# Attention of a two-layer kernel: head pairs, two-part fp32r operands and output groups of 256 queries

## What is computed

```python
qs = (x @ wq_sem).reshape(b, sl, H, DS)          # H = 16 heads, DS = DG = 64, DV = 128
ksem = (x @ wk_sem).reshape(b, sl, H, DS)
qg = _rope((x @ wq_geo).reshape(b, sl, H, DG))
kg = _rope((x @ wk_geo).reshape(b, sl, H, DG))
v = (x @ wv).reshape(b, sl, H, DV)
```

## Time and profile before

| | |
|---|---|
| median of 3 runs | 1966.86 us |
| the profiled execution | 1968.04 us, span 1966.4 us |
| PE busy / PE weight loads | 1781.5 us (91%) / 1315.6 us (67%) |
| DVE / ACT / POOL busy | 1106.4 us (56%) / 972.0 us (49%) / 802.1 us (41%) |
| mean granted clock of TensorE | 0.956 of full speed |

### The profile page before, as it was taken

The page is one execution under the profiler, slowest core; times in us unless marked ns, Lnnn a source line. Parts: engine busy times, 40 slices in busy tenths (PEclk is TensorE's granted clock), DMA queues, the critical chain, the costliest instruction groups (busy, mean ns, idle before and its releaser), DMA issues. The chain is left out here.

```text
span 1966.4 us, 33208 instructions
## 1 busy us (share of the span) xinstructions
PE 1781.5 (91%) x9018; PEld 1315.6 (67%) x9018; DVE 1106.4 (56%) x2157; ACT 972.0 (49%) x2052; POOL 802.1 (41%) x788
## 2 busy tenths in 40 slices
PE   6399988439999999999999999999999999999998
PEld 2256656427777777777777777777776677677777
DVE  4799953695546455554645454555544333334467
ACT  4599923015555555555555455555554344444322
POOL 1489931333433444343434434443432233222354
PEclk9599999559999999999999999999999999999999
DMA  4753258200000000000000000000101999999623
GB/s 138 287 183 105 98 154 261 84 3 20 9 20 16 21 8 19 16 20 7 16 21 8 19 16 21 8 19 16 39 9 31 286 313 314 308 315 321 192 87 97
DMA packets 99216, 192.94 MB, mean 98 GB/s; under 512 B 15332, under 2 KB 59620, under 8 KB 96596
## 3 DMA queue, kind: packets, MB, share of 16 engines
q1 hardware_dynamic: 57684, 108.76, 18.0%
q0 software_dynamic: 17152, 47.67, 7.5%
q10 hardware_dynamic: 24336, 35.98, 5.5%
HBM read 140.84 MB, written 51.51 MB: 98 GB/s over the span
## 5 line engine op out<-in xcount | busy, mean ns | idle before, releaser
L1175 POOL TENSOR_TENSOR sw<-sw,rope_t 64x512 f32<-64x512 f32 x128 | 164.3, 1283 | 611.9 <-ACT sw L995 611.9
L1078 DVE TENSOR_TENSOR t<-ps,rope_t 128x512 f32<-128x512 f32 x128 | 88.5, 692 | 363.5 <-ACT sw L995 363.4
L890 PE MATMUL ps<-pt,v 128*128 128x512 f32 (+3 forms) x768 | 270.1, 495 | 19.8 <-DVE xr L1095 17.8
L987 ACT ACTIVATE pb<-ps,negmax 128x128 f32<-128x128 f32 (+7 forms) x256 | 191.1, 747 | 177.1 <-DVE negmax L1063 177.0
L1063 DVE TENSOR_REDUCE negmax<-ps 128x1 f32<-128x128 f32 (+7 forms) x256 | 191.9, 750 | 78.1 <-PE ps L849 76.1
L890 PEld LDWEIGHTS ps<-pt,v 128*128 128x128 f32 x768 | 139.1, 191 | 121.4 <-issue 79.5
L541 POOL DMA_DIRECT2D w2r<-in_w x148 | 77.5, 523 | 326.1 <-PE ps L590 306.3
L1178 POOL TENSOR_TENSOR t<-t,sw 64x512 f32<-64x512 f32 x128 | 179.1, 1399 | 33.6 <-POOL sw L1175 17.9
L883 PE MATMUL ps<-ident,pb 128*128 128x128 f32 x1152 | 171.3, 276 | 23.6 <-ACT pb L987 23.4
L974 ACT COPY pt<-ps 128x512 f32<-128x512 f32 (+3 forms) x256 | 130.1, 508 | 102.0 <-PE ps L883 94.5
L883 PEld LDWEIGHTS ps<-ident,pb 128*128 128x128 f32 x1152 | 133.8, 141 | 68.1 <-ACT pb L987 45.1
(11 more groups left out here) (198 smaller groups left out, 3677.2 us busy)
## 6 DMA issues: line engine op xcount, KB each, us to landing
w13r<-in_w SPq DMA_DIRECT2D x124, 352.0 KB, 6.0
w2r<-in_w POOLq DMA_DIRECT2D x148, 176.0 KB, 6.0
result<-yy ACTq DMA_DIRECT2D x148, 128.0 KB, 5.1
crow<-c_rows SPq DMA_DIRECT2D x32, 512.0 KB, 3.6
t<-sorted SPq DMA_DIRECT2D x124, 128.0 KB, 5.5
sorted<-zeros ACTq DMA_DIRECT2D x15, 1024.0 KB, 16.9
hc<-in_w SPq DMA_DIRECT2D x24, 352.0 KB, 5.3
wraw<-in_wqkv SPq DMA_DIRECT2D x16, 384.0 KB, 3.3
```

The source lines that it names most:

```text
L890: last = pe.matmul(ps[:, 6, c0:512], v[:, buf, j], pt[g][:, j, c0:512], start=j == 0, stop=j == 4 * g + 3)
L987: act.activation(pb[:, qt % 2, 0:cols], ps[:, bank:bank + 2, :].rearrange("p a n -> p (a n)")[:, 0:cols], ACT.Exp, bias=negmax[:, par, qn: ...
L1175: g.tensor_tensor(sw[64:128, p % 2, :], sw[64:128, p % 2, :], rope_t[64:128, 1, (p // 2) * 512:(p // 2 + 1) * 512], ALU.mult).then_inc(s_t ...
```

## The change

The loop goes over pairs of heads, and inside a pair over four iterations c: sequence 0 with both heads, then sequence 1 with both heads (`hh` = c % 2 is the head within the pair, 1 the second one). There are still 32 iterations of eight steps, and maxima, exps, scores, transposes and pieces are as many and as large as before.

- Values are projected for both heads of a pair and 256 tokens at a time, in the iterations with hh = 0, steps 0, 1, 4 and 7, by `three` on the split x and split weights (12 matmuls of 256 columns each time).
- Probabilities are rounded to fp32r by ScalarE (all chunks, `ptr`), and VectorE subtracts to get the second part (`ptl`). A transpose chunk may overwrite its bank once that subtraction is done (`s_pl`). ScalarE does exp of tile qt + 1 before the copies of tile qt.
- Outputs are made in four groups of 256 queries per iteration, by `three`; each is rounded on ScalarE, split on VectorE, projected by `three` with a split wo, and added. All of it goes through bank 6, at fixed steps.
- The subtraction `rest` moves from VectorE to GpSimd, where it comes after the rotation of the following piece.
- Weights of the second head of a pair have their own slot; values and wo are split too. The loads are reordered accordingly.
- The ring buffer `w2r1` of the experts no longer has room of its own beside the attention's buffers; GpSimd waits for the end of attention before it loads it.

The core of the diff (lines removed from the printed functions are left out; "..." marks cuts):

```diff
+        early = {"w13r1": sbk("w13r1", [P, RING, DC, 2 * INNER]), "xs1": t1[:].rearrange("p a (b d) -> p (a b) d", d=D)}
...
+        vr = sbo("vr", [P, 8, 2 * P], F32R)
+        vl = sbo("vl", [P, 8, 2 * P], F32R)
+        ptr = [sbo("ptr0", [P, 6, 2 * P], F32R), sbo("ptr1", [P, 8, 2 * P], F32R)]
+        ptl = [sbo("ptl0", [P, 6, 2 * P], F32R), sbo("ptl1", [P, 8, 2 * P], F32R)]
...
+            def values(m, b, fill):
+                pe.wait_ge(s_e7, fill - 1)
+                for a in range(2):
+                    t0 = b * SEQ + (2 * m + a) * P
+                    o = ps[:, 7, a * 2 * P:(a + 1) * 2 * P]
                     for c in range(DC):
...
+                        last = three(pe, o, xnr[:, c, t0:t0 + P], xnl[:, c, t0:t0 + P], wvr[:, c], wvl[:, c], c == 0, c == DC - 1)
+                last.then_inc(s_b7, 1)
...
             def transposes(it, qt):
                 w(pe, s_exp, 8 * it + qt + 1)
                 for ci, j0, j1 in chunks(qt):
...
+                    w(pe, s_pl, CHUNKS * it + ci - 1)
                     for j in range(j0, j1):
                         last = pe.transpose(ps[:, 4 + ci % 2, (j - j0) * P:(j - j0 + 1) * P], pb[:, qt % 2, j * P:(j + 1) * P], ident[:])
                     last.then_inc(s_T, 1)
...
+            def output(it, g, hh):
+                w(pe, s_e6, output_fill(it, g) - 1)
+                pe.wait_ge(s_pl, CHUNKS * it + (2, 4, 8, 12)[g])
+                hd = slice(hh * P, (hh + 1) * P)
+                for j in range(2 * g + 2):
+                    c0 = P if j == 2 * g + 1 else 0
+                    last = three(pe, ps[:, 6, c0:2 * P], vr[:, j, hd], vl[:, j, hd], ptr[g % 2][:, j, c0:2 * P], ptl[g % 2][:, j, c0:2 * P],
+                                 j == 0, j == 2 * g + 1)
+                last.then_inc(s_b6, 1)
+            def project_out(it, g, slot):
+                pe.wait_ge(s_e6, project_fill(it, g) - 1)
                 for a in range(2):
...
+                    sl = slice(a * P, (a + 1) * P)
+                    last = three(pe, ps[:, 6, a * D:(a + 1) * D], otr[:, sl], otl[:, sl], wor[:, slot], wol[:, slot], True, True)
                 last.then_inc(s_b6, 1)
...
+            def body(hp, c, last):
+                it, pair = 4 * hp + c, 2 * hp + c // 2
+                b, hh = c // 2, c % 2
+                next_b = ((c + 1) % 4) // 2
                 for qt in range(8):
                     transposes(it, qt)
                     if qt < 6:
...
+                        scores(it, qt + 2, hh)
                     elif not last:
...
+                        scores(it, qt + 2, 1 - hh)
+                    if qt == 0 and not first(it):
+                        if hh == 1:
+                            pe.wait_ge(s_e7, value_fill(pair, 3))
+                        output(it - 1, 3, 1 - hh)
+                    if qt == 1 and not first(it):
+                        project_out(it - 1, 3, 1 - hh)
+                    if qt in (2, 4, 6):
+                        output(it, qt // 2 - 1, hh)
+                    if qt in (3, 5, 7):
+                        if qt == 3 and b == 0:
+                            pe.wait_ge(s_wos, 2 * hp + hh + 1)
+                        project_out(it, qt // 2 - 1, hh)
+                    if qt in VALUE and hh == 0:
+                        if qt == 0 and b == 0:
+                            pe.wait_ge(s_wvs, hp + 1)
+                        values(VALUE[qt], b, value_fill(pair, VALUE[qt]))
+                    if qt in PIECE and not last:
+                        p = PIECE[qt]
+                        if qt == 2 and next_b == 0:
+                            pe.wait_ge(s_ws, 2 * hp + c // 3 * 2 + (1 - hh) + 1)
+                        piece(p, next_b, 1 - hh, piece_fill(pair, hh, p))
             heads_loop(pe, body)
...
             def probs(it, qt):
...
+                for ci, j0, j1 in chunks(qt):
+                    act.wait_ge(s_T, CHUNKS * it + ci + 1)
+                    g = qt // 2
+                    if qt % 2 == 0 and j0 == 0:
+                        w(act, s_b6, output_fill(it, g - 2) if g >= 2 else output_fill(it - 1, g + 2))
+                    cols = slice((qt % 2) * P, (qt % 2 + 1) * P)
+                    act.copy(ptr[g % 2][:, j0:j1, cols], ps[:, 4 + ci % 2, 0:(j1 - j0) * P].rearrange("p (j q) -> p j q", q=P)).then_inc(s_pr, 1)
...
+            def body(hp, c, last):
+                it, pair, hh = 4 * hp + c, 2 * hp + c // 2, c % 2
                 n0 = 4 * (it + 1)
                 for qt in range(8):
+                    if qt < 7 or not last:
+                        exp_tile(it, qt + 1, hh)
                     probs(it, qt)
...
+                    if qt == 0 and not first(it):
+                        output(it - 1, 3)
+                    if qt in (2, 4, 6):
+                        output(it, qt // 2 - 1)
+                    if qt in VALUE and hh == 0:
+                        values(VALUE[qt], value_fill(pair, VALUE[qt]))
+                    if qt in PIECE and not last:
+                        p = PIECE[qt]
+                        swap(n0 + p, p, piece_fill(pair, hh, p))
                     if qt in (3, 4, 6, 7) and not last:
                         p = {3: 0, 4: 1, 6: 2, 7: 3}[qt]
...
             def probs(it, qt):
...
+                    dve.wait_ge(s_pr, CHUNKS * it + ci + 1)
+                    g = qt // 2
+                    o = (slice(None), slice(j0, j1), slice((qt % 2) * P, (qt % 2 + 1) * P))
+                    dve.tensor_tensor(ptl[g % 2][o], ps[:, 4 + ci % 2, 0:(j1 - j0) * P].rearrange("p (j q) -> p j q", q=P),
+                                      ptr[g % 2][o].bitcast(F32), ALU.subtract).then_inc(s_pl, 1)
...
+            def body(hp, c, last):
+                it, pair = 4 * hp + c, 2 * hp + c // 2
+                b, hh = c // 2, c % 2
+                prev_b = ((c + 3) % 4) // 2
                 n0 = 4 * (it + 1)
                 for qt in range(8):
                     if qt < 7 or not last:
...
+                        max_tile(it, qt + 1, hh)
+                    probs(it, qt)
                     if qt == 0 and not first(it):
...
+                        output(it - 1, 3)
+                    if qt == 1 and not first(it):
+                        add_out(it - 1, 3, prev_b, 1 - hh)
+                    if qt in (2, 4, 6):
+                        output(it, qt // 2 - 1)
+                    if qt in (3, 7):
+                        invert(it, qt // 7, hh)
+                    if qt in (3, 5, 7):
+                        add_out(it, qt // 2 - 1, b, hh)
+                    if qt in VALUE and hh == 0:
+                        values(VALUE[qt], 4 * pair + VALUE[qt] + 1)
+                    if qt in PIECE and not last:
+                        p = PIECE[qt]
                         turned(n0 + p, p)
...
+                    if qt == 1 and c == 2 and not last_pair(hp):
+                        dve.wait_ge(s_b7, piece_fill(pair - 1, 1, 3))
+                        split_qk(2 * hp + 2, 0)
+                    if qt == 1 and c == 3 and not last_pair(hp):
+                        dve.wait_ge(s_b7, first_fill(pair, V67))
+                        split_qk(2 * hp + 3, 1)
+                        split_values(hp + 1)
+                    if qt == 4 and c == 3 and not last_pair(hp):
+                        dve.wait_ge(s_b6, project_fill(it - 1, 3))
+                        split_wo(2 * hp + 2, 0)
+                    if qt == 4 and c == 0 and not first(it):
+                        dve.wait_ge(s_b6, project_fill(it - 1, 3))
+                        split_wo(2 * hp + 1, 1)
...
         def att_pool(g):
...
+            def rotate(it, p, fill):
                 n = 4 * it + p
+                w(g, s_ql, n if p == 0 else n - 1)
                 g.wait_ge(s_a7, n + 1)
                 g.tensor_tensor(sw[64:128, p % 2, :], sw[64:128, p % 2, :], rope_t[64:128, 1, (p // 2) * 512:(p // 2 + 1) * 512], ALU.mult).then_inc(s_t2, 1)
                 g.wait_ge(s_t2, n + 1)
...
+                g.wait_ge(s_e7, fill)
                 g.tensor_tensor(t1[64:128, p % 2, :], t1[64:128, p % 2, :], sw[64:128, p % 2, :], ALU.add).then_inc(s_rot, 1)
+            def rest(it, p, buf):
+                g.wait_ge(s_rot, 4 * it + min(p + 2, 4))
+                g.wait_ge(s_qr, 4 * it + p + 1)
+                o = (slice(None), buf, p % 2, slice((p // 2) * 512, (p // 2 + 1) * 512))
+                g.tensor_tensor(qkl[o], t1[:, p % 2, :], qkr[o].bitcast(F32), ALU.subtract).then_inc(s_ql, 1)
...
                     for p in range(4):
...
+                        rotate(it + 1, p, piece_fill(2 * hp + c // 2, c % 2, p))
+                        if p:
+                            rest(it + 1, p - 1, 1 - c % 2)
+                    rest(it + 1, 3, 1 - c % 2)
             heads_loop(g, body)
...
         def att_sp(sp):
...
+            load_qk(1)
+            load_wo(1)
+            with sp.Fori(0, PAIRS_H - 1) as hp:
+                load_qk(2 * hp + 2)
+                load_qk(2 * hp + 3)
```

(55 more changed lines are left out.)

286 lines of the change are left out of this document (107 added, 179 removed).

## The result

| | before | after |
|---|---|---|
| median | 1966.8 us (4 runs) | 2297.8 us (4 runs, 2291.4 to 2302.2) |
| ratio to the kernel before | 1 | 1.168 [1.165, 1.172] |
| span of the profiled execution | 1966.4 us | 2298.6 us |
| first exp of attention to first matmul of the experts | 445.4 to 1524.1, 1078.7 us | 442.9 to 1840.9, 1398.0 us |

The change makes the kernel 331 us slower. Of the 332 us between the two spans, attention has 319.3, which is 10.3 us for each of 31 iterations; the stretch ahead of it is 2.5 us shorter, the experts' 15.4 us longer. The last figure says little: over the twelve kernels of this study that stretch lasts 429 to 458 us, in no order with the edits. So the table of experiments gives attention's own time too.

A forecast was written before the change was run, and what follows sets the result against it. TensorE's in-order queue was taken to bound the kernel. Per iteration 30.8 + 5.0 + 4.5 + 2.8 = 43.1 us, less 33.54 = 9.5, times 31 = 295: 1968 + 295 = 2263 us, range 2125 to 2340.

The forecast's parts named there:

- TensorE's own work: Attention's matmuls: 15.07 us removed and 13.7 added per iteration, so a fall of 1.4 to 30.8 us.
- The moved subtraction: Step 6, scores at qt = 8: TensorE stands still 5.0 us (4.9 to 6.1) per iteration for GpSimd's second rest.
- The clock: Behind the 5 us wait, work runs at half rate for about 5.7 us, costing 2.8 us per iteration (0 to 5.6).
- the range's upper bound: 2340 us in total, where shorter waits in attention lower TensorE's clock too.
- The chain: Longer loop of maximum, exp, copy and subtraction between ScalarE and VectorE: TensorE waits 4.5 us per iteration (1.3 to 7).
- At no cost: Weight loads and GpSimd's scattering cost nothing; -2 us ahead of attention and +2 at the experts cancel.
- The -2 ahead of attention: Ahead of the first iteration `v_half` goes and VectorE's splits of the second head replace it: -2 us.
- +2: The later `w2r` load delays the experts' first down projection: 2 us more.
- Rival (a): In attention the clock holds: 40.3 us per iteration, 2178 us in total; chance 0.2.
- (b): At qt = 8 the wait for rest 1 is covered: 35.3 us per iteration, 2023 us in total; chance 0.07.
- (c): Faster: TensorE's queue stays full in attention, 32.1 us per iteration, 1925 us in total; chance 0.05.
- (d): Attention's new products cost more than 0.12 us each, for instance bound by weight loads; called hardly likely, no separate chance.

The follow-up runs named there:

- e9: e5 with VectorE's maximum taken one step earlier, ahead of the turned piece; 1937 us, ratio 0.990 to the kernel before.
- e2: The changed kernel with 18 unused matmuls of 512 columns just ahead of TensorE's wait at qt = 8; 2207 us, ratio 1.127 to the kernel before.
- e1: The changed kernel with GpSimd's order made rotate 0, rotate 1, rest 0, rest 1, then likewise 2 and 3; 2097 us, ratio 1.074 to the kernel before.
- e6: The changed kernel with only the loop over head pairs written out; ratio 1.158 to the kernel before.
- e5: e1 with ScalarE's copies before the next tile's exp and the loop over head pairs written out; 1972 us, ratio 1.002 to the kernel before.
- e7: The kernel before with two heads (four iterations) per loop round instead of one; ratio 1.000 to the kernel before.

## Why the prediction was right, and where its terms were not

- **TensorE's own work** was forecast to fall by only 1.4 us per iteration. It holds: matmuls of 256 columns start 0.12 us apart in the new products. In e9 attention is 25.7 us shorter than before, so an iteration lasts 32.7 us; its three rows above are 53.5 us of waits in 24.5 iterations, 2.2 us each, which leaves 30.5 against 30.8.
- **The moved subtraction.** Place, path and size are as forecast: 5.4 us from the piece to the scores against 5.7, a subtraction of 1.27 us against 1.3, a wait of 4.3 us against 5.0 (the transposes ahead of it took 1.0 us, not 0.7). GpSimd's time also agrees better with the estimate from rows than with the 1.4 us by the Trainium skill (GPSIMD Engine Reference, Key points), which says that VectorE is about twice as fast: this subtraction took 0.69 us there before the change and takes 1.27 on GpSimd, a factor of 1.85.
- **The clock** was to cost 2.8 us per iteration, for 5.7 us of work at half rate behind the wait. Removing its fall there gave 2.1 to 2.4 (e2), and the low stretches behind the 22 waits last 5.9 us on average, part of it before TensorE resumes. That the clock also falls after shorter waits, 1.81 and 0.74 us in a row, was the range's upper bound, and happened, in every second iteration. This is the term that was mis-sized: a mean clock of 0.91 is 180 us at half rate in 1000, 7.9 us in each of the 22.8 iterations, which costs up to 4.0 us instead of 2.8.
- Wait and clock together were put at 7.8 us; the reordering that removes both gave 6.1 (e1).
- **The chain** was put at 4.5 us, and its size held: the changed kernel's rows other than those for L1216 and "issue" are 98.7 us in 22.8 iterations, 4.3 us each, and e1's are 123.1 us in 26.5 iterations, 4.6 each. Its places did not: the hand schedule took it at three, and e1's list has 97 waits for L1089 in 26 iterations, almost four in each. That e1's iteration is 7.0 us above TensorE's own 30.8 isn't the chain alone: 1.0 us are "issue" waits and up to 0.8 is its clock of 0.98; some 0.6 us is in no row.
- **Jumps back** were not in the sum: writing out the loop gave 0.6 to 0.9 us per iteration (e6, e5). The changed kernel's "issue" waits are 0.4 us of it.
- "At no cost" held for the weights' loads (no DMA wait in attention). The -2 ahead of attention is there (2.5 us shorter). For the experts' `w2r` +2 was right in kind: the first down projection waited 3.61 us for it. What else makes up the experts' 15.4 us is open.

With what the rows show, the sum is 30.8 + 4.2 for the wait + 4.3 for the chain + 0.4 for the "issue" waits + up to 4.0 for the clock = 43.7 us. 43.1 us were forecast and 33.54 + 10.3 = 43.8 measured, 2263 against 2298 us. So the mechanisms were right, but that the total came so close is partly luck: a wait 0.8 us too long made up for most of a clock 1.2 us too cheap. Rival (a), clock holds, fell with the mean clock of 0.91 and with e2; (b) and (c), the wait covered, and (d), dearer products, fell with the first trace.

## What to carry to other kernels

When an operation moves to another engine's queue, look for the last thing that stands ahead of it there: here a subtraction that was ready early stood behind one that needed the piece just computed, and its reader came next. Cheaper products on the bounding engine gain nothing if its partners' chains grow to its length; take the long-latency step (here the maximum) ahead of whatever waits for other engines. Price a wait of some microseconds on TensorE with the slow matmuls behind it, too.

## What the runs showed of the hardware that was not expected

- 18 useless matmuls per iteration made the kernel some 80 us faster (e2), since they kept the clock up behind the wait.
- A loop body of four iterations of the changed kernel is fetched more than once: its first instruction queue moves 1.34 MB, and 1.08 with the loop written out. At the start of a round TensorE stands for some 2 us in the changed kernel and some 5 in e1, and in e5 and e6, without the loop, it doesn't. Four iterations of the kernel before, which have fewer instructions (5194 TensorE matmuls in 29.8 iterations of the earlier trace rows, 174 each, against 4822 in 22.8, some 211 each), show no such wait on TensorE (e7), but neither does e2, with more. What decides whether TensorE stands there is open.
